# Where a transformer block's SyncE queue issues five kinds of transfers around its first gate-and-up stage

## The chip, the cores and the metric

The kernel runs on one core of a Trainium2 chip as one launch. The metric is the device time in microseconds (us); the kernel before took 1146.49 us as the median of three runs (1145.63 to 1148.01). The engines are TensorE (PE, with its weight loads PEld apart), VectorE (DVE), ScalarE (ACT), GpSimd (POOL) and SyncE (SP). Here SP issues every DMA transfer of the kernel.

## The reference

One transformer block with modulated layer norms, linear attention and a feed-forward part whose weights are 4-bit indices into a table of 16 values. x is 2 x 2048 x 512 in float32, there are 16 heads of 32, and the inner width is 1376.

```python
h = _layernorm(x) * (1 + ca) + sa
q = heads(h @ q_w.T + q_b); k = heads(h @ k_w.T + k_b); v = heads(h @ v_w.T + v_b)
qp = elu(q) + 1; kp = elu(k) + 1
kv = einsum('bhsd,bhse->bhde', kp, v)                  # a sum over the whole sequence
z  = einsum('bhsd,bhd->bhs', qp, kp.sum(axis=2))
x  = x + ga * ((einsum('bhsd,bhde->bhse', qp, kv) / (z + 1e-6)) @ o_w.T + o_b)
h  = _layernorm(x) * (1 + cb) + sb
x  = x + gb * ((silu(h @ lut[gate_idx].T) * (h @ lut[up_idx].T)) @ lut[down_idx].T)
```

sa, ca, ga, sb, cb, gb come from silu(c) @ wmod. Since kv is a sum over the sequence, no row can be finished before every row of its batch has been read once.

## The kernel before

The 4096 rows are cut into 8 groups of 512. Matrices are split into a high and a low half-precision part, and one product is three matmuls: high x high (L1437), high x low (L1438), low x high (L1439). A product of a 128-wide chunk of the inner width with one group is 12 such matmuls of 128x512.

Stage A goes through the 8 groups once for q, k, v and the kv sums, and stores each group's q to `qp_dram`. Then come eight gate-and-up stages `stage_b(s)`, and last a down stage. The inner width has 11 chunks (`FC`), the last of 96 rows. The first stage, s = 0, has 9 chunks (`HELD`), j = 0 to 8 of group 0; below they are called e0 to e8, and e9 on are the chunks of the next stage. Between the chunks of stage s the attention of group s + 1 is finished: its q is divided by z, multiplied with the output weights (`o_piece`, four products of 12 matmuls), normalised and turned (`t_piece`). In stage 0 part of the attention of group 2 is done as well.

One chunk e runs through five engines, each in an order written out by hand:

- PE: 12 matmuls for the gate, 12 for the up product, in banks that alternate with e.
- ACT `silu_gate` (L837): silu of the gate's bank.
- DVE `hid_full` (L1281): `hid_f[e % 2]` = silu times up. It waits for the up product, for silu, and from e2 on for the landing of the store that last read this half of `hid_f`, that of e - 2 (`full_out[e % 2]`).
- ACT `hid_hi` (L845): the high part of `hid_f`; POOL `hid_lo` (L631): the low part.
- SP: a store of `hid_f` to `full_dram` (L496) when `hid_f` is done, and a store of both parts to `hid_dram` (L498) when the low part is done.

Between these stand the attention's instructions. For group 1 in stage 0 they are: DVE `qn_full(1, c)` (L1223) for its four pieces c, ACT `qn_hi` (L776), POOL `qn_lo` (L592). ACT does `qn_hi(1, 2)` and `qn_hi(1, 3)` after `silu_gate` of e3, which stands behind `hid_hi` of e2. POOL does `qn_lo(1, 2)` and `qn_lo(1, 3)` behind `hid_lo` of e2. PE's `o_piece(1, 0)`, behind the up product of e3, waits for all four `qn_lo` of group 1:

```python
if t == 0:
    pe.wait_ge(m_ready, b + 1)
    pe.wait_ge(qn_done, 4 * n + 8)
```

SP's program is one list too, and an instruction of it that waits holds up all that stand behind it. At the end of stage A it stores the last group's q (L402), waits until that store has landed, loads group 2's q (L422) and the output weights for batch 1 (L423), and stores group 0's x after the attention (L427, `x1_store`). Then follow the chunks: before e3's stores the load of the next x into `xg[0]` (L433, `x_next`), and before e4's stores 11 loads of down indices (L474). The first half of `hid_f` is stored again and again under one pair of semaphores:

```python
sp.wait_ge(hid_f_done, e + 1)
if j < FC - 1:
    sp.dma_start(full_dram[g][:, j], hid_f[:, e % 2]).then_inc(full_out[e % 2], 16)
sp.wait_ge(hid_done, e + 1)
sp.dma_start(hid_dram[g][0:m, j], hid[0:m, e % HIDS]).then_inc(hid_out[e % HIDS], 16)
```

Who needs the moved transfers: group 2's q is scaled by ACT `qs_all(2)` (L762) after `hid_hi` of e3; the output weights are read by PE in the middle of stage 1; the x loaded by `x_next(0, 0)` is read by POOL at the start of stage 1; DVE waits for the down indices at the start of stage 2. The down indices go to a part of `w_ffn` that group 0's and group 1's early q and normalised rows use up to e2, so SP waits for those (`x2T_done`, `qn_f_done`) before it loads them.

Of the kernel before, what the change touches and what calls it, by code (L numbers as in the profile page):

```python
# [34 lines left out]
P = 128  # L35
# [13 lines left out]
FC = -(-INTER // P)  # L49
# [30 lines left out]
LOOK_B = [[([(p, False) for p in pieces], first, shares) for pieces, first, shares in stage] for stage in LOOK_B]  # L80
UNITS = [u for units in LOOK_A for u in units] + [u for stage in LOOK_B for units, _, _ in stage for u in units]
EARLY_J = 7


HELD = FC - 2
# [25 lines left out]
def adaln_kernel(nc, x, qwT, qb, kwT, kb, vwT, vb, owT, ob, lut, gateT, upT, downT, cT, wmod, out):  # L111
    with ExitStack() as ctx:
        def sb(name, shape, dt):
            return ctx.enter_context(nc.sbuf_tensor(name, shape, dt))

        def sem(name):
            return ctx.enter_context(nc.semaphore(name))

        def part(arena, start, dt, *dims):

            n = 1
            for d in dims:
                n *= d
            words = n * (2 if dt == F16 else 4) // 4
            v = arena[:, start:start + words]
            if dt != U32:
                v = v.bitcast(dt)
            if len(dims) == 2:
                v = v.rearrange("p (a b) -> p a b", a=dims[0])
            elif len(dims) == 3:  # L130
                v = v.rearrange("p (a b c) -> p a b c", a=dims[0], b=dims[1])
            elif len(dims) == 4:
                v = v.rearrange("p (a b c d) -> p a b c d", a=dims[0], b=dims[1], c=dims[2])
            return v
# [14 lines left out]
        down_idx = w_ffn[:, GU * GROUP:PIECES * GROUP].bitcast(I32).rearrange("p (j n) -> p j n", j=FC)  # L149
# [10 lines left out]
        owt = [qn_words.bitcast(F32).rearrange("p (k n) -> p k n", k=KC), part(arena, 3 * tile_w, F32, KC, HID)]  # L160
# [12 lines left out]
        qp = sb("qp", [P, KC, GROUP], F32)  # L173
# [75 lines left out]
        qp_dram = nc.dram_tensor("qp_dram", (GROUPS, P, KC * GROUP), F32, kind="Internal").ap()  # L249
# [5 lines left out]
        def sems(names):  # L255
            return (sem(n) for n in names.split())
# [3 lines left out]
        idx_in = [sem(f"idx{i}_in") for i in range(5)]  # L260
        raw_in = [sem(f"raw{n}_in") for n in "kvq"]
        mod_in = [sem(f"mod{m}_in") for m in range(6)]
        ow_in = [sem("ow0_in"), sem("ow1_in")]
# [13 lines left out]
        q_neg, q_read, q_act, qp_done, qp_out = sems("q_neg q_read q_act qp_done qp_out")  # L277
# [8 lines left out]
        q_in, qs_done, z_done, z_read, rec_done, spread_done, qn_f_done, qn_hi_done, qn_done = sems(  # L286
            "q_in qs_done z_done z_read rec_done spread_done qn_f_done qn_hi_done qn_done")
        o_done, xob_done, x1_done, stats2_raw, stats2_done, ve2_done, rstd2_done, nmr2_done, xn2_done = sems(
            "o_done xob_done x1_done stats2_raw stats2_done ve2_done rstd2_done nmr2_done xn2_done")
        x2T_done, h2_f_done, h2_done = sems("x2T_done h2_f_done h2_done")  # L290
# [16 lines left out]
        def chunked(w, k=KC):  # L307
            return w.rearrange("(k p) n -> p k n", k=k)

        def flat(v):  # L310
            return v.rearrange("p k n -> p (k n)")
# [4 lines left out]
        def rows_of(j):  # L316
            return P if j < FC - 1 else TAIL
# [35 lines left out]
        def _(sp):  # L353
# [43 lines left out]
            def stage_a(g, par, load):  # L397
                if load:
                    sp.wait_ge(xT_done, 4 * g + 4)
                    sp.dma_start(xg[:, par], xv[g + 2]).then_inc(x_in[par], 16)  # L400
                sp.wait_ge(qp_done, 4 * g + 8)
                sp.dma_start(qp_dram[g], flat(qp[:])).then_inc(qp_out, 16)  # L402
# [15 lines left out]
            sp.wait_ge(xT_done, 4 * 7 + 4)  # L418
            sp.dma_start(xg[:, 1], xv[1]).then_inc(x_in[1], 16)
            stage_a(7, 1, False)  # L420
            sp.wait_ge(qp_out, 16 * 8 + 16)
            sp.dma_start(flat(qp[:]), qp_dram[2]).then_inc(q_in, 16)  # L422
            sp.dma_start(owt[1], chunked(owT)).then_inc(ow_in[1], 16)  # L423

            def x1_store(n, par):
                sp.wait_ge(x1_done, 4 * n + 4)
                sp.dma_start(x1_dram[n], flat(xg[:, par])).then_inc(x1_out[par], 16)  # L427

            def x_next(n, par):
                sp.wait_ge(xn2_done, 4 * n + 4)  # L430
                sp.wait_ge(x1_out[par], 16 * (n // 2 + 1))
                if n + 2 < GROUPS:
                    sp.dma_start(xg[:, par], xv[n + 2]).then_inc(x_in[par], 16)  # L433
                else:
                    sp.dma_start(flat(xg[:, par]), x1_dram[n + 2 - GROUPS]).then_inc(x1_in[par], 16)

            def q_next(n):
                sp.wait_ge(qn_f_done, 4 * n)
                sp.dma_start(flat(qp[:]), qp_dram[n]).then_inc(q_in, 16)

            def full_load(u):
                g, i, cols = u // 2, u % 2, slice(u % 2 * UNIT, u % 2 * UNIT + UNIT)
                if i == 0:
                    for s, count in full_landed(SLOT[(g, FC - 1)]):
                        sp.wait_ge(s, count)
                if u >= 2:
                    sp.wait_ge(left_summed, 4 * (u - 1))
                sp.dma_start(hid_raw[i], full_dram[g][:, :, cols]).then_inc(full_in[i], 16)

            def hid_load(u):  # L450
                g, i, t = u // 2, u % 2, 2 * (u % 2)
                if i == 0:
                    for s, count in landed(SLOT[(g, FC - 1)]):
                        sp.wait_ge(s, count)
                if u >= 2:
                    sp.wait_ge(prod_ready, 7 * (u - 1))
                for which, k, tile in ((S_A11, 0, t), (S_A12, HALF_K, t), (S_A22, HALF_K, t + 1)):
                    sp.dma_start(left[i][which], hid_dram[g][:, k:k + HALF_K, tile]).then_inc(hid_in[i], 16)
                sp.dma_start(left_last[i][0:TAIL], hid_dram[g][0:TAIL, FC - 1, t:t + 2]).then_inc(hid_in[i], 16)

            x1_store(0, 0)
            for s in range(GROUPS):
                n = s + 1
                store, nxt = (6, 7) if s == 0 else (3, 5)
                for i, (g, j) in enumerate(STAGES[s]):
                    e, m = SLOT[(g, j)], rows_of(j)
                    if s == 0 and i == 3:
                        x_next(0, 0)
                    if s == 0 and i == 4:
                        sp.wait_ge(x2T_done, 8)  # L470
                        sp.wait_ge(qn_f_done, 8)
                        for jd in range(FC):
                            md = rows_of(jd)
                            sp.dma_start(down_idx[0:md, jd], downT[jd * P:jd * P + md, :]).then_inc(idx_in[4], 16)  # L474
                    if s < GROUPS - 1:
                        if i == store:
                            x1_store(n, n % 2)
                        if i == nxt:
                            x_next(n, n % 2)
                        if i == 8 and n + 2 < GROUPS:  # L480
                            q_next(n + 2)
                    elif i == 1:
                        sp.wait_ge(up_done, SLOT[(GROUPS - 1, 0)] + 1)
                        hid_load(0)
                    elif i == 5:
                        sp.wait_ge(wf_done, 2 * HALF_K)
                        sp.wait_ge(b_planes, 3 * HALF_K + 1)
                        full_load(0)
                    elif i == 7:
                        sp.wait_ge(up_done, SLOT[(GROUPS - 1, 4)] + 1)  # L490
                        hid_load(1)
                    elif i == 8:
                        full_load(1)
# [5 lines that stand above are left out]
# [930 lines left out]
        def _(pe):  # L1429
# [290 lines left out]
            def gate(g, j):  # L1720
                e = SLOT[(g, j)]
                if j >= EARLY_J:
                    pe.wait_ge(gu_ready, j - EARLY_J + 1)
                if e >= 2:
# [123 lines left out]
```

## Time and profile before

| | before |
|---|---|
| time, median of 3 runs (lowest to highest) | 1146.49 us (1145.63 to 1148.01) |
| the profiled execution's own time | 1147.93 us |
| its span, from the first to the last instruction | 1145.7 us |
| busy: PE, DVE, ACT, POOL | 1105.9, 867.5, 516.8, 370.6 us |
| mean granted TensorE clock | 0.992 |
| the chain that ended last, by engine | PE 84%, DVE 7%, issue 4%, ACT 3% |
| DMA: moved, mean rate over the span | 162.79 MB, 142 GB/s |

The span is what the profile covers; the execution's own time holds some 2 us more. "Busy" of PE counts matmuls, which overlap. The granted clock is the share of full speed at which TensorE was let run. In a timeline, the bracket at a row's end is the time that the engine sat idle before it, and what the profile takes for the releaser; "issue" says that the profile saw none. A transfer's time to landing runs from its issue by SP to the landing of its last part. Stage 0 begins on PE with e0's gate at 355.3 us; DVE multiplies its last chunk, e8, at 432.2 us.

### The profile page before, as it was taken

To read this page: it belongs to the slowest core of one execution; us is meant where nothing else is said; L and a number is where in the kernel's file an instruction comes from. 1 tells how busy PE (TensorE), PEld (TensorE's weight loads), DVE (VectorE), ACT (ScalarE), POOL (GpSimd) and SP (SyncE) were. 2 spreads that over 40 slices of the span, in tenths; PEclk is the share of its full clock that TensorE was granted. 3 is DMA by queue.
4 is the path that set the end of the run, shared out by engine and by line. 5 is a ranking of instruction groups with operands and counts; after the bars stand their busy time and mean duration, and the time that the engine had idled before them with its cause. 6 is when DMAs were issued, how large, how long until landed. Compare 5 with 4: busy or idle time off the path is not lost.

```text
span 1145.7 us, 19116 instructions
## 1 busy us (share of the span) xinstructions
PE 1105.9 (97%) x7508; PEld 610.2 (53%) x7534; DVE 867.5 (76%) x1251; ACT 516.8 (45%) x877; POOL 370.6 (32%) x331
## 2 busy tenths in 40 slices
PE   4899999999999799999999999999999999999998
PEld 2344444544444344444544444444444468888887
DVE  4688988776779568898766987956743968887884
ACT  4667787777726233242421423324224742333231
POOL 1000100002115255474722735726434222222222
PEclk9899999999999899999999999999999999999999
DMA  7930231123112843333322414323242466888872
GB/s 270 324 123 20 89 111 67 46 74 111 37 39 80 276 148 102 138 111 117 127 106 94 157 72 152 113 110 117 76 155 82 158 224 218 257 278 280 272 253 101
DMA packets 115736, 162.79 MB, mean 142 GB/s; under 512 B 7520, under 2 KB 70496, under 8 KB 111552
## 3 DMA queue, kind: packets, MB, share of 16 engines
q1 hardware_dynamic: 115648, 161.58, 41.9%
q8 instruction: 59, 0.97, 0.4%
q14 instruction: 29, 0.24, 0.1%
HBM read 92.88 MB, written 68.68 MB: 141 GB/s over the span
## 4 chain that ended last, share of the span: by engine, by line
PE 84%; DVE 7%; issue 4%; ACT 3%; POOL 1%; DMA 1%; SPq 0%; POOLq 0%; DVEq 0%; ACTq 0%
PE bank L1437 20%; PE bank L1439 20%; PE bank L1438 20%; PE bank L1753 5%; PE bank L1754 5%; PE bank L1755 5%; PE bank L1445 2%; DVE look_buf L1116 2%; PE bank L1589 1%; DMA w_ffn<-in_wmod 1%; DVE w_ffn L1116 1%; PE bank L1507 1%; PE bank L1571 1%; PE bank L1550 1%; PE bank L1757 1%
## 5 line engine op out<-in xcount | busy, mean ns | idle before, releaser
L631 POOL TENSOR_TENSOR shared<-hid_f,shared 128x512 f16<-128x512 f32 (+1 forms) x88 | 117.6, 1336 | 279.2 <-ACT shared L845 279.1
L1437 PE MATMUL bank<-h,w_ffn 128*128 128x512 f16 (+1 forms) x528 | 200.4, 379 | 0.3 <-POOL h L610 0.3
L1438 PE MATMUL bank<-h,w_ffn 128*128 128x512 f16 (+1 forms) x528 | 200.1, 379 | 0.0
L1439 PE MATMUL bank<-h,w_ffn 128*128 128x512 f16 (+1 forms) x528 | 200.1, 379 | 0.0
L845 ACT ACTIVATE shared<-hid_f 128x512 f16<-128x512 f32 (+1 forms) x88 | 55.5, 630 | 249.4 <-DVE hid_f L1281 249.2
L1281 DVE SCALAR_TENSOR_TENSOR hid_f<-bank,sc,shared 128x512 f32<-128x512 f32 (+1 forms) x88 | 65.6, 746 | 100.1 <-PE bank L1439 40.8
L1437 PE MATMUL bank<-arena,h 128*128 128x512 f16 x256 | 98.8, 386 | 5.7 <-issue 2.7
L837 ACT ACTIVATE shared<-bank,sc 128x512 f32<-128x512 f32 (+1 forms) x88 | 60.1, 683 | 96.8 <-PE bank L1439 96.4
L1113 DVE TENSOR_SCALAR look_buf<-look_buf,tab_x,tab 128x512 uint32<-128x512 uint32 x147 | 101.0, 711 | 0.6
L1438 PE MATMUL bank<-arena,h 128*128 128x512 f16 x256 | 98.3, 384 | 0.0
L1439 PE MATMUL bank<-arena,h 128*128 128x512 f16 x256 | 98.3, 384 | 0.0
L639 POOL TENSOR_TENSOR xg<-xg,shared 128x512 f32<-128x512 f32 x32 | 47.7, 1492 | 155.3 <-DVE shared L1353 155.3
L1437 PEld LDWEIGHTS bank<-h,w_ffn 128*128 128x128 f16 (+1 forms) x528 | 52.9, 100 | 66.6 <-issue 8.6
L1116 DVE COPY_PREDICATED look_buf<-look_buf 128x512 uint32<-128x512 uint32 x84 | 85.7, 1020 | 1.2
L1439 PEld LDWEIGHTS bank<-h,w_ffn 128*128 128x128 f16 (+1 forms) x528 | 52.9, 100 | 61.0
L1438 PEld LDWEIGHTS bank<-h,w_ffn 128*128 128x128 f16 (+1 forms) x528 | 52.9, 100 | 57.3 <-issue 0.3
L1116 DVE COPY_PREDICATED w_ffn<-look_buf 128x512 uint32<-128x512 uint32 (+1 forms) x69 | 68.9, 999 | 0.9
L885 ACT ACTIVATE qn_f<-bank,sc 128x256 f32<-128x256 f32 x32 | 14.9, 466 | 120.2 <-PE bank L1755 120.2
L559 POOL TENSOR_SCALAR stats<-stats 128x4 f32<-128x4 f32 x7 | 4.9, 698 | 198.2 <-ACT h L721 198.2
L1437 PE MATMUL bank<-arena,w_ffn 128*128 128x512 f16 (+1 forms) x176 | 66.7, 379 | 0.0
L1438 PE MATMUL bank<-arena,w_ffn 128*128 128x512 f16 (+1 forms) x176 | 66.7, 379 | 0.0
L1439 PE MATMUL bank<-arena,w_ffn 128*128 128x512 f16 (+1 forms) x176 | 66.7, 379 | 0.0
(287 smaller groups left out, 2606.2 us busy)
## 6 DMA issues: line engine op xcount, KB each, us to landing
full_dram<-hid_f SPq DMA_DIRECT2D x80, 256.0 KB, 2.0
hid_dram<-shared SPq DMA_DIRECT2D x80, 256.0 KB, 2.0
w_ffn<-full_dram SPq DMA_DIRECT2D x16, 1280.0 KB, 9.9
xg<-in_x SPq DMA_DIRECT2D x16, 1024.0 KB, 7.0
qp_dram<-qp SPq DMA_DIRECT2D x8, 1024.0 KB, 4.9
x_dram<-xg SPq DMA_DIRECT2D x8, 1024.0 KB, 4.1
xg<-x_dram SPq DMA_DIRECT2D x8, 1024.0 KB, 7.2
qn<-hid_dram SPq DMA_DIRECT2D x24, 320.0 KB, 4.0
```

Source lines behind the costliest of these rows:

```text
L631: pool.tensor_tensor(hid[0:m, e % HIDS, :, 1], whole, hid[0:m, e % HIDS, :, 0], ALU.subtract).then_inc(hid_done, 1)
L837: act.activation(silu_g[0:m, e % 2], bank[2 + 2 * (e % 2)][0:m], ACT.Silu, scale=c1(C_INV_G)[0:m]).then_inc(silu_g_done, 1)
L845: act.activation(hid[0:m, e % HIDS, :, 0], whole, ACT.Copy).then_inc(hid_hi_done, 1)
L1113: ins = dve.tensor_scalar(buf(dst), buf("m0"), tab_x[:, a:a + 1], tab[:, 2 * a:2 * a + 1], ALU.bitwise_and, ALU.bitwise_xor)
L1116: ins = dve.copy_predicated(buf(dst), buf(a), buf(b))
L1281: dve.scalar_tensor_tensor(hid_f[0:m, i], bank[3 + 2 * i][0:m], c1(C_HID)[0:m], silu_g[0:m, i], ALU.mult, ALU.mult).then_inc(hid_f_done, 1)
L1437: pe.matmul(dst, a_hi, b_hi, start=first, stop=False)
L1438: pe.matmul(dst, a_hi, b_lo, start=False, stop=False)
L1439: last = pe.matmul(dst, a_lo, b_hi, start=False, stop=end)
L1753: pe.matmul(dst, l[:, jj, 0], r[:, jj, 0], start=start and jj == 0, stop=False, skip_group_check=True)
L1754: pe.matmul(dst, l[:, jj, 0], r[:, jj, 1], start=False, stop=False, skip_group_check=True)
L1755: last = pe.matmul(dst, l[:, jj, 1], r[:, jj, 0], start=False, stop=end, skip_group_check=True)
```

## The change

Only SP's list changes; PE, DVE, ACT and POOL keep their instructions and their order. A new table `DOWN_LOADS` says before which chunk's stores which down chunks are loaded.

```diff
+DOWN_LOADS = {(0, 5): (0, 1), (0, 6): (2, 3), (0, 7): (4, 5), (0, 8): (6, 7), (1, 0): (8,), (1, 1): (9,), (1, 2): (10,)}
...
             stage_a(7, 1, False)
-            sp.wait_ge(qp_out, 16 * 8 + 16)
-            sp.dma_start(flat(qp[:]), qp_dram[2]).then_inc(q_in, 16)
-            sp.dma_start(owt[1], chunked(owT)).then_inc(ow_in[1], 16)
...
-            x1_store(0, 0)
             for s in range(GROUPS):
                 n = s + 1
                 store, nxt = (6, 7) if s == 0 else (3, 5)
                 for i, (g, j) in enumerate(STAGES[s]):
                     e, m = SLOT[(g, j)], rows_of(j)
-                    if s == 0 and i == 3:
-                        x_next(0, 0)
-                    if s == 0 and i == 4:
-                        sp.wait_ge(x2T_done, 8)
-                        sp.wait_ge(qn_f_done, 8)
-                        for jd in range(FC):
-                            md = rows_of(jd)
-                            sp.dma_start(down_idx[0:md, jd], downT[jd * P:jd * P + md, :]).then_inc(idx_in[4], 16)
+                    if s == 0:
+                        if i == 1:
+                            sp.wait_ge(qp_out, 16 * 8 + 16)
+                            sp.dma_start(flat(qp[:]), qp_dram[2]).then_inc(q_in, 16)
+                        elif i == 2:
+                            x1_store(0, 0)
+                        elif i == 3:
+                            sp.dma_start(owt[1], chunked(owT)).then_inc(ow_in[1], 16)
+                        elif i == 4:
+                            x_next(0, 0)
+                        elif i == 5:
+                            sp.wait_ge(x2T_done, 8)
+                            sp.wait_ge(qn_f_done, 8)
+                    for jd in DOWN_LOADS.get((s, i), ()):
+                        md = rows_of(jd)
+                        sp.dma_start(down_idx[0:md, jd], downT[jd * P:jd * P + md, :]).then_inc(idx_in[4], 16)
```

On SP, from the last store of stage A to the first store of chunk e0, the list stood so before (L402 the last q store, L422 group 2's q, L423 the output weights, L427 group 0's x, L496 and L498 the two stores of e0):

```order
L402 DMA qp_dram<-qp 128x2048
L422 DMA qp<-qp_dram 128x2048
L423 DMA arena<-in_owT 128x4x512
L427 DMA x_dram<-xg 128x2048
L496 DMA full_dram<-hid_f 128x512
L498 DMA hid_dram<-shared 128x1024
```

The same place now, from the last store of stage A (L405) to the first store of chunk e3; line numbers are those of the changed file, in which L503 and L505 are the two stores of a chunk:

```order
L405 DMA qp_dram<-qp 128x2048
L503 DMA full_dram<-hid_f 128x512
L505 DMA hid_dram<-shared 128x1024
L469 DMA qp<-qp_dram 128x2048
L503 DMA full_dram<-hid_f 128x512
L505 DMA hid_dram<-shared 128x1024
L427 DMA x_dram<-xg 128x2048
L503 DMA full_dram<-hid_f 128x512
L505 DMA hid_dram<-shared 128x1024
L473 DMA arena<-in_owT 128x4x512
L503 DMA full_dram<-hid_f 128x512
```

The two stores of e0 moved ahead of three 1 MB transfers, and ahead of SP's wait for the last q store; the stores of e1 stand behind one of the three, those of e2 behind two.

The second place on SP is where the next x and the down indices are loaded. Before, from the load of x (L433) on, chunks e3 and e4:

```order
L433 DMA xg<-in_x 128x4x512
L496 DMA full_dram<-hid_f 128x512
L498 DMA hid_dram<-shared 128x1024
L474 DMA w_ffn<-in_downT 128x512 x10
L474 DMA w_ffn<-in_downT 96x512
L496 DMA full_dram<-hid_f 128x512
```

Now, from the load of x on, chunks e4 to e7 (L481 loads down indices, L427 stores group 1's x, L433 loads the x after it):

```order
L433 DMA xg<-in_x 128x4x512
L503 DMA full_dram<-hid_f 128x512
L505 DMA hid_dram<-shared 128x1024
L481 DMA w_ffn<-in_downT 128x512 x2
L503 DMA full_dram<-hid_f 128x512
L505 DMA hid_dram<-shared 128x1024
L481 DMA w_ffn<-in_downT 128x512 x2
L427 DMA x_dram<-xg 128x2048
L503 DMA full_dram<-hid_f 128x512
L505 DMA hid_dram<-shared 128x1024
L481 DMA w_ffn<-in_downT 128x512 x2
L433 DMA xg<-in_x 128x4x512
```

The 11 loads in one row became two before each of e5 to e8 and one before each of e9 to e11; the load of x stands one chunk later.

## Rows read from the trace of the kernel before

**Rows 1.** The page's part 1: busy us (share of the span) xinstructions.
```profile
PE 1105.9 (97%) x7508; PEld 610.2 (53%) x7534; DVE 867.5 (76%) x1251; ACT 516.8 (45%) x877; POOL 370.6 (32%) x331
```

**Rows 2.** Timeline of PE, e2's gate to e4's: start, us, engine, line, op.
```profile
370.78 0.38 PE L1439 MATMUL bank<-h,w_ffn 128*128 128x512 f16 x1
...
379.71 0.38 PE L1439 MATMUL bank<-h,w_ffn 128*128 128x512 f16 x1
386.66 0.59 PE L1437 MATMUL bank<-arena,qn 128*128 128x512 f16 x1 [6.57 <-issue]
...
391.39 0.38 PE L1437 MATMUL bank<-h,w_ffn 128*128 128x512 f16 x1
...
393.99 0.38 PE L1437 MATMUL bank<-arena,qn 128*128 128x512 f16 x1
```

**Rows 3.** Two stretches: us, busy by engine (x), PEclk, DMA share, GB/s.
```profile
386.66:391.39 4.73, 4.73 (x12) 1.72 (x13) 1.12 (x2) 3.08 (x5) 1.15 (x1) 0.54 0.92 316
421.16:426.00 4.84, 4.84 (x25) 2.47 (x26) 1.49 (x3) 3.19 (x6) 2.24 (x2) 1.00 0.54 171
```

**Rows 4.** Timeline of DVE: the last two pieces of q, then e2's product.
```profile
374.86 0.69 DVE L1223 SCALAR_TENSOR_TENSOR qn_f<-w_ffn,bank 128x512 f32<-128x512 f32 x1 [0.43 <-POOL qn L592]
380.88 0.75 DVE L1281 SCALAR_TENSOR_TENSOR hid_f<-bank,sc,shared 128x512 f32<-128x512 f32 x1 [5.34 <-DMA full_dram<-hid_f]
```

**Rows 5.** Timeline of SP's queue: issue, us that the issue took.
```profile
367.17 0.34 SPq L422 DMA_DIRECT2D qp<-qp_dram  x1
...
368.57 0.77 SPq L496 DMA_DIRECT2D full_dram<-hid_f  x1
...
390.13 6.22 SPq L474 DMA_DIRECT2D w_ffn<-in_downT  x11
```

**Rows 6.** DMA issues of 362 to 384 us: KB each, median us to landing.
```profile
qp<-qp_dram SPq DMA_DIRECT2D x1, 1024.0 KB, 4.8
arena<-in_owT SPq DMA_DIRECT2D x1, 1024.0 KB, 8.8
...
full_dram<-hid_f SPq DMA_DIRECT2D x3, 256.0 KB, 12.1
```

**Rows 7.** The page's part 6, whole span: the same store.
```profile
full_dram<-hid_f SPq DMA_DIRECT2D x80, 256.0 KB, 2.0
```

**Rows 8.** Timeline of ACT, e2's silu to the scaling of group 2's q.
```profile
371.20 0.69 ACT L837 ACTIVATE shared<-bank,sc 128x512 f32<-128x512 f32 x1 [2.27 <-PE bank L1439]
...
381.67 0.63 ACT L845 ACTIVATE shared<-hid_f 128x512 f16<-128x512 f32 x1 [8.75 <-DVE hid_f L1281]
382.21 0.67 ACT L837 ACTIVATE shared<-bank,sc 128x512 f32<-128x512 f32 x1
382.77 1.14 ACT L776 ACTIVATE qn<-qn_f 128x512 f16<-128x512 f32 x2
...
388.35 2.55 ACT L762 ACTIVATE qp<-qp,ksq 128x512 f32<-128x512 f32 x4
```

**Rows 9.** Timeline of POOL in the same stretch.
```profile
372.48 2.27 POOL L592 TENSOR_TENSOR qn<-qn_f,qn 128x512 f16<-128x512 f32 x2 [2.32 <-ACT qn L776]
382.38 1.33 POOL L631 TENSOR_TENSOR shared<-hid_f,shared 128x512 f16<-128x512 f32 x1 [7.62 <-ACT shared L845]
383.67 2.89 POOL L592 TENSOR_TENSOR qn<-qn_f,qn 128x512 f16<-128x512 f32 x2
```

**Rows 10.** Timeline of PE: two other idle times, in stage A and stage 0.
```profile
39.95 0.63 PE L1437 MATMUL bank<-arena,h 128*128 128x512 f16 x1 [2.71 <-issue]
...
421.16 0.66 PE L1445 MATMUL bank<-ident,arena 128*128 128x128 f32 x4 [1.40 <-POOL arena L605]
```

**Rows 11.** The store of e7 alone (line L496, 425.2 to 425.6 us).
```profile
L496 SPq DMA_DIRECT2D full_dram<-hid_f x1: 319/319/319, 425.3 to 425.3; - x1
...
DMA to landing us min/median/max: 3.6/3.6/3.6
```

**Rows 12.** Timeline of DVE: e9's product, two chunks after that store.
```profile
438.52 0.73 DVE L1281 SCALAR_TENSOR_TENSOR hid_f<-bank,sc,shared 128x512 f32<-128x512 f32 x1
```

## The prediction

> **What bounds the kernel now.** I read the page's busy times first: PE is busy in 97% of the span [rows 1], so only PE's idle time, and the time in which it runs slowly, can move the end. Second came PE's timeline, stretch by stretch, to list its idle times. After stage A has begun in earnest there are few, and one stands out [rows 2]: the up product of e3 ends at 379.71 + 0.38 = 380.09 us, and the next matmul, the first of `o_piece(1, 0)`, starts at 386.66. The reader is to see the bracket of 6.57 us, and that the 12 matmuls of that product take 391.39 - 386.66 = 4.73 us, where the next 12 take 393.99 - 391.39 = 2.60. Third, the stretches by granted clock: it is 0.54 for those 12 and 1.00 at 421 us [rows 3], so they ran mostly at 1.2 GHz and not at 2.4, after an idle engine. So one place costs 6.57 + 2.13 = 8.70 us.
>
> "Issue" names no cause, so I went back along the program. `o_piece(1, 0)` waits for the last `qn_lo` on POOL, which ends at 383.67 + 2.89 = 386.56, 0.10 before PE starts [rows 9]. It waited for ACT's `qn_hi` at 382.77, that stood behind `hid_hi` of e2 at 381.67 [rows 8], and that waited for DVE's product of e2 at 380.88. DVE had been free since 374.86 + 0.69 = 375.55 and sat idle for 5.34 us until a DMA landed [rows 4]: the store of e0's `hid_f`. SP issued it at 368.57, after it had waited until 367.17 for the last q store and had then issued three transfers of 1 MB [rows 5]. It took 12.1 us to land, behind them [rows 6], where the median of all 80 such stores is 2.0 [rows 7]: 368.57 + 12.1 = 380.7, and DVE starts at 380.88.
>
> **The change, part by part.** *Stores of e0 ahead of the burst.* SP now issues e0's store as soon as e0's product is done, before it waits for the q store. That product precedes 367.17 (SP found it done). In front of the store is only the last q store, and that had landed by 367.17. So e0's store lands at the latest a little after 367.17 + 2.0 = 369.2, against the 375.55 at which DVE wants it: the 5.34 us go. Bounds: with the 12.1 us of before, from about 364 it would be 376.1, a wait of 0.6.
>
> What is late next, step by step. DVE begins e2's product at 375.6; its up product ended 24 matmuls before e3's, at 380.09 - 2 x 2.60 = 374.9, so PE is not the limit. ACT's `hid_hi` follows 0.79 later (381.67 - 380.88), at 376.4, and ends by 377.0. `silu_gate` of e3 then waits for e3's gate, which ends at 380.09 - 2.60 = 377.5; on e2 ACT began 0.04 after the gate's end (371.20 against 370.78 + 0.38), so ACT is there at 377.5 instead of 382.21. The `qn_hi` pair begins 0.56 after it (382.77 - 382.21), at 378.1, and the first of the two ends half of 1.14 later, at 378.7. POOL has `hid_lo` of e2 from 377.1 (0.71 after `hid_hi`) to 378.4, so its `qn_lo` pair begins at about 378.8, with 0.1 for the handoff. The pair took 2.27 at 372.48 and 2.89 at 383.67 [rows 9]. I take 2.89, since DVE's table lookups run beside it as they did there; 2.27 is the other end. It ends at 381.7, and PE starts at 381.8: 4.9 us earlier than 386.66, with an idle time of 1.7 left. At the other end it is 5.5.
>
> *The clock.* An idle time of 1.40 at 421.16 was followed by a stretch at 1.00 [rows 3, 10]; one of 2.71 at 39.95 was followed by matmuls of 0.63 us, as at 386.66, against 0.38 [rows 2, 10]. 1.7 is nearer to 1.40, so I take the clock as kept: 2.13 us are saved, at the other end nothing.
>
> *Stores of e1 and e2.* e1's store stands behind group 2's q (1 MB, 4.8 us to landing [rows 6]), issued at 367.17 as before. It lands at about 374, and even with 12.1 us at about 381. The product of e3 wants it when e3's up product is done, at 380.1, and DVE's lookups run until about 382: no cost at either end. e2's stores stand behind group 0's x, which SP issues at about 370.7; two chunks later there is ample room.
>
> *Output weights before e3, next x before e4.* e3's store is issued behind the output weights, which took 8.8 us beside two other transfers [rows 6]. e5's product is two chunks and three products of `o_piece` after e3's: seven times 2.60, some 18 us, against 12.1. No cost. The next x is issued behind the landed x store, that SP waits for; SP reaches it after e3's low part, some 13 us after that store's issue, more than 12.1.
>
> *Down loads in pairs.* The 11 loads took SP 6.22 us to issue and held up nothing that PE waited for [rows 5]; taking them apart gives nothing. They now stand before the stores of e5 to e11. The tightest store I found is e7's: issued at 425.3, landed in 3.6 us [rows 11], wanted by e9's product at 438.52 [rows 12], 13.2 us after its issue. Two loads are 0.5 MB; the 3.25 MB of the burst took from 367.17 to 380.7, so 0.5 MB are about 2.1 us. 5.7 against 13.2: no cost. Each later time is shifted alike on all engines, since from 386.66 on they wait for PE.
>
> *Issuing later.* Group 2's q leaves SP at 367.17 as before, lands at 367.17 + 4.8 = 372.0, and ACT takes it up at 388.35 [rows 8], after the change at about 383. It stays early by some 10 us. The Trainium skill, DMA: Bandwidth & Descriptors, in Rules for kernel authors, says to issue a DMA early and to wait on it late, which speaks against moving loads back. By that rule alone the sum would be 0 or a loss, and it is weighed as the last rival below; the trace differs here, since the early burst is what DVE's 5.34 us waited behind.
>
> **The sum.** 4.9 + 2.1 = 7.0 us. The profiled execution took 1147.93 us, with a span of 1145.7: it would take 1140.9. It was 1.4 us above the median of 1146.49, so in terms of the median I forecast 1139.5 us.
>
> **The rivals.**
> - *The clock falls all the same.* The 1.7 us left are more than the 1.40 that did no harm, and some step of the chain may be slower than I took it. Then the gain is 4.9 and the time 1141.6; with an idle time of 2.7, 3.9 and 1142.6. For it: 2.71 was enough once. Against: the steps are measured ones.
> - *The idle time goes entirely*, if POOL's pair is fast and ACT overlaps more: 8.7 us, 1137.8. Against it: e3's gate ends at 377.5, and four steps follow it.
> - *Nothing changes.* e0's store still lands late, or another wait of the same length takes its place, since POOL or SP is later than I think: about 1146.5. Against: it would have to land 11 us after its issue, with one transfer in front of it.
> - *Slower: the paired loads make landings late in several chunks.* Place: DVE's products of e8 to e11, which wait for stores that now have down loads, an x store, an x load or a q load in front of them. The point from which it decides is 13.2 us to landing. At 16 us each of four chunks would lose 2.8, 11.2 in all, and with the 7.0 saved the time is 1150.7. Against: 5.7 was worked out, and the stores that had 3 MB in front took 12.1.
>
> **How the numbers follow.** Forecast 0.71, clock falls 0.13, idle gone 0.08, nothing changes 0.04, slower 0.04. The first three are faster, 0.92 together; 0.2% is 2.3 us, about what a measurement here can tell from no change. The range goes from 1137.4, which is the case without idle time less 0.4 for the spread of runs, to 1142.4, which takes in most of the case with the low clock; outside are the last two and a part of the second, under 0.2.
>
> **What would show it.** In the profile after: e0's store issued at about 364 and landed by 370; no DVE idle time on a DMA before e2's product, which starts at about 375.6; PE's idle time before `o_piece(1, 0)` at 1 to 2 us and its 12 matmuls in 2.6 us at a granted clock of 1.00; the idle time of 1.40 before `t_piece(1, 0)` as before, some 7 us earlier. I am wrong if DVE waits for a landing at e3, e8, e9 or e10, if PE's 12 matmuls still take 4.7 us, or if PE gets a new idle time later in stages 0 and 1.

## The result, and the profile after

The changed kernel took 1138.94 us as the median of four runs (1138.04 to 1141.27), against 1146.06 us of the kernel before in the four runs taken by then (1145.07 to 1148.01). The ratio is 0.9939, with a 95% interval of 0.9918 to 0.9960: faster by 7.1 us, where 7.0 were forecast (1139.5 us in terms of the median). The profiled execution took 1141.27 us with a span of 1139.0.

PE after the change, from the end of e3's up product on (columns as before: start, us, engine, line; L1444 to L1446 are the L1437 to L1439 of before):

```profile
379.94 0.38 PE L1446 MATMUL bank<-h,w_ffn 128*128 128x512 f16 x1
382.11 0.38 PE L1444 MATMUL bank<-arena,qn 128*128 128x512 f16 x1 [1.80 <-issue]
...
384.70 0.38 PE L1444 MATMUL bank<-h,w_ffn 128*128 128x512 f16 x1
...
414.47 0.65 PE L1452 MATMUL bank<-ident,arena 128*128 128x128 f32 x4 [1.40 <-POOL arena L612]
```

These answer to [rows 2]: the idle time of 6.57 us is down to 1.80, and the 12 matmuls of `o_piece(1, 0)` take 384.70 - 382.11 = 2.59 us instead of 4.73. The idle time of 1.40 before `t_piece(1, 0)` [rows 10] is still there, 6.7 us earlier. The granted clock of the same stretches, against [rows 3], where the first had 0.54 (columns: stretch, us, then busy time of PE, PEld, DVE, ACT, POOL, granted clock, DMA share, GB/s):

```profile
382.11:384.70 2.59, 2.59 (x13) 1.17 (x13) 0.00 (x0) 2.59 (x5) 1.16 (x1) 1.00 0.94 361
414.47:419.00 4.53, 4.53 (x24) 2.35 (x24) 1.19 (x3) 2.88 (x5) 2.22 (x2) 1.00 0.56 176
```

SP's queue, answering to [rows 5], and the landing of e0's store of `hid_f` alone. It answers to the 12.1 us of [rows 6], which is the median of three stores; e0's alone took 12.2 before:

```profile
363.51 0.34 SPq L405 DMA_DIRECT2D qp_dram<-qp  x1
364.18 0.34 SPq L503 DMA_DIRECT2D full_dram<-hid_f  x1
...
367.42 0.32 SPq L469 DMA_DIRECT2D qp<-qp_dram  x1
368.51 0.32 SPq L503 DMA_DIRECT2D full_dram<-hid_f  x1
```

```profile
L503 SPq DMA_DIRECT2D full_dram<-hid_f x1: 338/338/338, 364.2 to 364.2; - x1
...
DMA to landing us min/median/max: 3.9/3.9/3.9
```

It leaves SP at 364.18, as soon as e0's product is done, and lands at 368.1. In the kernel before, the last q store left at 363.30 and e0's product was done just as early, at 363.19 + 0.74 = 363.93, but SP issued the store only at 368.57 [rows 5]:

```profile
363.30 0.34 SPq L402 DMA_DIRECT2D qp_dram<-qp  x1
```

```profile
363.19 0.74 DVE L1281 SCALAR_TENSOR_TENSOR hid_f<-bank,sc,shared 128x512 f32<-128x512 f32 x1
```

```profile
L496 SPq DMA_DIRECT2D full_dram<-hid_f x1: 773/773/773, 368.6 to 368.6; - x1
...
DMA to landing us min/median/max: 12.2/12.2/12.2
```

So, counted from the issue of the last q store, the landing comes 12.9 us sooner: 4.6 because the store is issued sooner, 8.3 because it lands sooner after its issue. DVE, answering to [rows 4], no longer waits:

```profile
375.08 0.69 DVE L1230 SCALAR_TENSOR_TENSOR qn_f<-w_ffn,bank 128x512 f32<-128x512 f32 x1 [0.43 <-POOL qn L599]
375.68 0.75 DVE L1288 SCALAR_TENSOR_TENSOR hid_f<-bank,sc,shared 128x512 f32<-128x512 f32 x1
...
380.93 0.73 DVE L1288 SCALAR_TENSOR_TENSOR hid_f<-bank,sc,shared 128x512 f32<-128x512 f32 x1
```

And the steps behind it, ACT's (`hid_hi` of e2, `silu_gate` of e3, the `qn_hi` pair) and POOL's (`hid_lo` of e2, the `qn_lo` pair), against [rows 8, 9]:

```profile
376.46 0.63 ACT L852 ACTIVATE shared<-hid_f 128x512 f16<-128x512 f32 x1 [3.32 <-DVE hid_f L1288]
377.76 0.69 ACT L844 ACTIVATE shared<-bank,sc 128x512 f32<-128x512 f32 x1 [0.67 <-PE bank L1446]
378.35 1.14 ACT L783 ACTIVATE qn<-qn_f 128x512 f16<-128x512 f32 x2
```

```profile
377.17 1.35 POOL L638 TENSOR_TENSOR shared<-hid_f,shared 128x512 f16<-128x512 f32 x1 [2.19 <-ACT shared L852]
379.04 2.97 POOL L599 TENSOR_TENSOR qn<-qn_f,qn 128x512 f16<-128x512 f32 x2 [0.52 <-ACT qn L783]
```

What the reader is to see is the releaser of `silu_gate`: it is now PE, so the chain starts at e3's gate product, and POOL's pair ends at 382.01, 0.10 before PE goes on.

Spans are hard to compare directly, since stage A's start differs by up to 3 us between executions: the last q store leaves SP at 360.58 to 363.51 us in the profiles of this study. So I take the time from that store to the end of the span. Before it is 1145.7 - 363.3 = 782.4, after it is 1139.0 - 363.5 = 775.5: 6.9 us. The two terms read above are (6.57 - 1.80) + (4.73 - 2.59) = 4.77 + 2.14 = 6.91, the same within the 0.1 us to which spans are given.

### The profile page after: what moved, and what is told of

It reads as the page before. It is cut to its first block, busy times and chain, and to the rows that moved or that the text cites. A ratio compares the mean times of both kernels' runs of the same rounds, so it can differ in the third digit from the quotient of the medians.

```text
span 1139.0 us, 19142 instructions
## 1 busy us (share of the span) xinstructions
PE 1106.0 (97%) x7534; PEld 609.5 (54%) x7534; DVE 866.5 (76%) x1251; ACT 517.1 (45%) x877; POOL 370.6 (33%) x331
## 4 chain that ended last, share of the span: by engine, by line
PE 85%; DVE 7%; issue 3%; ACT 3%; POOL 1%; DMA 1%; SPq 0%; POOLq 0%; DVEq 0%; ACTq 0%
PE bank L1444 20%; PE bank L1446 20%; PE bank L1445 20%; PE bank L1760 5%; PE bank L1761 5%; PE bank L1762 5%; PE bank L1452 2%; DVE look_buf L1123 2%; PE bank L1596 1%; DMA w_ffn<-in_wmod 1%; DVE w_ffn L1123 1%; PE bank L1514 1%; PE bank L1578 1%; PE bank L1557 1%; PE bank L1764 1%
## 5 line engine op out<-in xcount | busy, mean ns | idle before, releaser
L1444 PE MATMUL bank<-h,w_ffn 128*128 128x512 f16 (+1 forms) x528 | 200.4, 379 | 0.2 <-POOL h L617 0.2
L1446 PE MATMUL bank<-h,w_ffn 128*128 128x512 f16 (+1 forms) x528 | 200.1, 379 | 0.0
L1444 PE MATMUL bank<-arena,h 128*128 128x512 f16 x256 | 98.9, 386 | 2.1 <-DVE h L1029 1.1
L1446 PE MATMUL bank<-arena,h 128*128 128x512 f16 x256 | 98.3, 384 | 0.0
L1444 PEld LDWEIGHTS bank<-h,w_ffn 128*128 128x128 f16 (+1 forms) x528 | 52.9, 100 | 66.8 <-issue 8.6
L1446 PEld LDWEIGHTS bank<-h,w_ffn 128*128 128x128 f16 (+1 forms) x528 | 52.9, 100 | 61.1
L1444 PE MATMUL bank<-arena,w_ffn 128*128 128x512 f16 (+1 forms) x176 | 66.7, 379 | 0.0
L1446 PE MATMUL bank<-arena,w_ffn 128*128 128x512 f16 (+1 forms) x176 | 66.7, 379 | 0.0
```

Of the source, the lines that this page charges most:

```text
L1444: pe.matmul(dst, a_hi, b_hi, start=first, stop=False)
L1446: last = pe.matmul(dst, a_lo, b_hi, start=False, stop=end)
```

## The experiments

The runs are numbered 1 to 9, while e0, e1 and so on stay the names of chunks. Each run was timed in turn with the kernel before. The table gives the ratio to it with the 95% interval, and from each profile DVE's wait for the store of e0, PE's idle time before `o_piece(1, 0)`, the time of its 12 matmuls, and the time from the last q store to the end. The first two rows are the kernels before and after. The edits of runs 1, 6, 7 and 9 are shown against the changed kernel, the others against the kernel before.

| kernel | ratio | DVE waits | PE idle | 12 matmuls | q store to end |
|---|---|---|---|---|---|
| before | 1 | 5.34 | 6.57 | 4.73 | 782.4 |
| after | 0.9939 [0.9918, 0.9960] | 0 | 1.80 | 2.59 | 775.5 |
| run 1, first burst alone | 0.9949 [0.9936, 0.9962] | 0 | 1.80 | 2.59 | 775.5 |
| run 2, down loads alone | 0.9996 [0.9987, 1.0005] | 5.06 | 6.29 | 4.83 | 782.3 |
| run 3, e0's stores first | 0.9944 [0.9930, 0.9958] | 0 | 1.80 | 2.59 | 775.6 |
| run 4, 2 MB ahead | 0.9938 [0.9927, 0.9950] | 1.36 | 2.62 | 2.59 | 776.3 |
| run 8, 2.5 MB ahead | 0.9990 [0.9980, 1.0000] | 3.82 | 5.04 | 4.22 | 780.4 |
| run 5, on ACT's queue | 0.9944 [0.9932, 0.9956] | 0.72 | 2.41 | 2.59 | 776.1 |
| run 9, down loads before e7 | 0.9932 [0.9918, 0.9946] | 0 | 1.78 | 2.59 | 775.5 |

In every row the last column is 775.5 plus what idle time and matmuls have over 1.80 and 2.59, within 0.1 us. The ratios of runs 1, 3, 4, 5, 9 and of the changed kernel cannot be told apart; by their profiles, one of each, runs 1, 3 and 9 are like the changed kernel, and runs 4 and 5 are 0.8 and 0.6 us slower. Runs 6 and 7 are below.

**Run 1: the first burst alone dealt out.**

```diff
-DOWN_LOADS = {(0, 5): (0, 1), (0, 6): (2, 3), ...
+DOWN_LOADS = {(0, 4): tuple(range(FC))}
...
+                        if i == 3:
+                            x_next(0, 0)
                         elif i == 4:
-                            x_next(0, 0)
-                        elif i == 5:
                             sp.wait_ge(x2T_done, 8)
```

> Only the first burst is dealt out (group 2's q before e1, group 0's x before e2, output weights before e3); the next x stands before e3 and the 11 down loads in a row before e4, as in the kernel before. Theory (all of the gain comes from e0's stores no longer standing behind 3 MB): as the changed kernel, 1138.9 us, PE idle before o_piece(1, 0) 1.8 us at a granted clock of 1.00. Rival (the second burst costs something too): 1 to 3 us slower than the changed kernel, with a new idle time of DVE on a landing at e5 or e6.

Measured: 1141.11 us against 1147.62 of the kernel before, and the same 775.5 as after. DVE waits for no landing at e5 or e6. The times alone would not exclude the rival's loss of 1 us, since the ratios 0.9949 and 0.9939 have intervals that overlap; the profile does, and by it the theory holds.

**Run 2: the down loads alone dealt out**, with the load of the next x moved as in the change.

```diff
-                    if s == 0 and i == 3:
+                    if s == 0 and i == 4:
                         x_next(0, 0)
-                    if s == 0 and i == 4:
+                    if s == 0 and i == 5:
                         sp.wait_ge(x2T_done, 8)
                         sp.wait_ge(qn_f_done, 8)
-                        for jd in range(FC):
...
+                    for jd in DOWN_LOADS.get((s, i), ()):
```

> Only the second burst is dealt out (next x before e4, down loads in pairs from e5 on); the first burst stays ahead of e0's stores. Theory: as the kernel before, 1146.1 us within 0.2%, PE idle 6.6 us before o_piece(1, 0), DVE idle 5.3 us on the landing of e0's store. Rival (the second burst costs something): 1 to 3 us faster than before.

Measured: 1146.51 against 1147.62, no difference. DVE before e2's product, and PE before `o_piece(1, 0)`:

```profile
379.32 0.75 DVE L1282 SCALAR_TENSOR_TENSOR hid_f<-bank,sc,shared 128x512 f32<-128x512 f32 x1 [5.06 <-DMA full_dram<-hid_f]
```

```profile
385.11 0.58 PE L1438 MATMUL bank<-arena,qn 128*128 128x512 f16 x1 [6.29 <-issue]
```

The stall is as it was. The half of the change that moves the most transfers is worth nothing.

**Run 3: the first burst kept whole, but behind e0's stores.**

```diff
-            sp.wait_ge(qp_out, 16 * 8 + 16)
-            sp.dma_start(flat(qp[:]), qp_dram[2]).then_inc(q_in, 16)
-            sp.dma_start(owt[1], chunked(owT)).then_inc(ow_in[1], 16)
...
-            x1_store(0, 0)
...
+                    if s == 0 and i == 1:
+                        sp.wait_ge(qp_out, 16 * 8 + 16)
+                        sp.dma_start(flat(qp[:]), qp_dram[2]).then_inc(q_in, 16)
+                        sp.dma_start(owt[1], chunked(owT)).then_inc(ow_in[1], 16)
+                        x1_store(0, 0)
```

> The first burst is kept whole, as three transfers in a row with the wait for the last q store ahead of them, but e0's two stores stand ahead of it instead of behind it; all else as in the kernel before. Theory (one store's place is the whole effect): as the changed kernel, 1139 us; e0's store lands by 369; e1's and e2's stores, now behind 3 MB, land at about 381, when e3's product is ready anyway (e3's product at 381, e4's at 393). Rival (spreading is what helps, since the burst now delays e1's store): DVE waits for e1's store until about 381.5 and later work slips, 1141 to 1146 us.

Measured: 1140.32 against 1147.62. This is the clearest of the runs, since the burst is untouched. e1's store now stands behind the 3 MB and lands as late as e0's did; then DVE's products of e2 and e3:

```profile
L497 SPq DMA_DIRECT2D full_dram<-hid_f x1: 602/602/602, 366.1 to 366.1; - x1
...
DMA to landing us min/median/max: 12.2/12.2/12.2
```

```profile
372.91 0.75 DVE L1282 SCALAR_TENSOR_TENSOR hid_f<-bank,sc,shared 128x512 f32<-128x512 f32 x1
...
378.36 0.75 DVE L1282 SCALAR_TENSOR_TENSOR hid_f<-bank,sc,shared 128x512 f32<-128x512 f32 x1
```

The landing at 366.1 + 12.2 = 378.3 comes just ahead of e3's product at 378.36. The same 12.2 us that cost 7 us on e0's store cost nothing on e1's. Dealing out is not what helps; the place of e0's stores is.

**Runs 4 and 8: how much stands ahead of e0's stores.** Run 4 stores group 0's x behind them; run 8 in place of that loads the second half of the output weights behind them, between the stores of e0 and e1.

```diff
-            x1_store(0, 0)
             for s in range(GROUPS):
...
+                    if s == 0 and i == 1:
+                        x1_store(0, 0)
```

```diff
-            sp.dma_start(owt[1], chunked(owT)).then_inc(ow_in[1], 16)
+            sp.dma_start(owt[1][:, 0:2], chunked(owT)[:, 0:2]).then_inc(ow_in[1], 16)
...
+                    if s == 0 and i == 1:
+                        sp.dma_start(owt[1][:, 2:4], chunked(owT)[:, 2:4]).then_inc(ow_in[1], 16)
...
-                    pe.wait_ge(ow_in[b], 16)
+                    pe.wait_ge(ow_in[b], 16 + 16 * b)
```

> The kernel before with two transfers of 1 MB ahead of e0's stores in place of three (group 0's x is stored behind e0's stores). A dose: 3.25 MB took from 367.2 to 380.8, so 2.25 MB take 9.4 us. Theory: e0's store lands at about 376.6 to 377.5, DVE idle 1 to 2 us before e2's product, PE idle 2.8 to 3.8 us before o_piece(1, 0), which is 1 to 2 us over the 1.8 of the changed kernel; with the clock kept 1140 to 1141 us, with the clock lost for one product 1142 to 1143. Rival (the wait does not go with the bytes in front): 1139 or 1146.

> The kernel before, with the second half of the output weights' load (0.5 MB) behind e0's stores, so 2.5 MB stand ahead of them; 2 MB gave DVE 1.36 us and PE 2.62 us of idle time, 3 MB gave 5.34 and 6.57. Theory (the wait goes with the bytes in front): DVE idle 3.0 to 3.7 us, PE idle 4.2 to 5.0. If the clock is kept after that, 2.7 us slower than the changed kernel, 1141.6; if it falls for o_piece(1, 0), 4.2 to 4.9 slower, 1143 to 1144. Rival (steps, not bytes): as with 2 or with 3 transfers.

Measured: run 4 1140.35 against 1147.62, run 8 1144.97 against 1146.65. DVE and PE of run 4, then of run 8, with the stretch of run 8's 12 matmuls:

```profile
375.38 0.75 DVE L1282 SCALAR_TENSOR_TENSOR hid_f<-bank,sc,shared 128x512 f32<-128x512 f32 x1 [1.36 <-DMA full_dram<-hid_f]
```

```profile
381.18 0.38 PE L1438 MATMUL bank<-arena,qn 128*128 128x512 f16 x1 [2.62 <-issue]
```

```profile
378.26 0.75 DVE L1283 SCALAR_TENSOR_TENSOR hid_f<-bank,sc,shared 128x512 f32<-128x512 f32 x1 [3.82 <-DMA full_dram<-hid_f]
```

```profile
384.04 0.59 PE L1439 MATMUL bank<-arena,qn 128*128 128x512 f16 x1 [5.04 <-issue]
```

```profile
384.04:388.26 4.22, 4.22 (x12) 1.55 (x13) 1.11 (x2) 3.07 (x5) 1.15 (x1) 0.60 0.80 304
```

The wait goes with the bytes ahead: e0's store lands 8.8, 10.7 and 12.2 us after its issue, and DVE waits 1.36, 3.82 and 5.34 us, at 2, 2.5 and 3 MB. SP's wait for the last q store alone is not the cause, for in runs 4 and 8 it still stands ahead of e0's store. Run 4 came within its expectation but for PE's idle time, 0.2 below it. In run 8 both idle times came out slightly above what I expected (3.0 to 3.7 and 4.2 to 5.0), and with them the loss against the changed kernel: 780.4 - 775.5 = 4.9 us, at the upper end of the 4.2 to 4.9 expected. Here the longer idle time cost more than its length: after 2.62 us the matmuls start 0.22 apart as ever, after 5.04 the first eight run at 1.2 GHz, and 1.63 us are lost to that beside the idle time. In time run 8 is close to the kernel before, and its interval reaches 1.0000; the runs alone do not show a gain, and its size is read from the profile, 780.4 against 782.4.

**Run 5: e0's store on ACT's queue, no sooner than before.** SP counts a semaphore up once it has issued the three transfers, and ACT waits for that; SP leaves this one store out.

```diff
+            sp.sem_inc(burst_issued, 1)
...
-                    if j < FC - 1:
+                    if j < FC - 1 and e:
...
+                    if s == 0 and i == 1:
+                        act.wait_ge(hid_f_done, 1)
+                        act.wait_ge(burst_issued, 1)
+                        act.dma_start(full_dram[0][:, 0], hid_f[:, 0]).then_inc(full_out[0], 16)
```

> The kernel before, with one store issued elsewhere: e0's store of hid_f goes out on ACT's queue, and not before SP has issued its three transfers of 1 MB, so the same 3 MB are under way and only the queue differs. Theory as the prediction had it (a store lands behind the bytes that were issued before it, whoever issues it): it lands after about 12 us, DVE idle 5 us, 1146 us. Rival (it waits only behind what stands in its own queue, and the 16 DMA engines serve both queues in turn): it lands in 2 to 5 us, DVE does not wait, PE idle 1.8 us before o_piece(1, 0), 1139 to 1140 us; e1's store stays behind the burst and costs nothing.

Measured: 1139.57 against 1146.65. The issues of 362 to 386 us (KB each, median us to landing), and DVE's product of e2:

```profile
x_dram<-xg SPq DMA_DIRECT2D x1, 1024.0 KB, 12.6
...
full_dram<-hid_f ACTq DMA_DIRECT2D x1, 256.0 KB, 7.9
```

```profile
374.02 0.75 DVE L1287 SCALAR_TENSOR_TENSOR hid_f<-bank,sc,shared 128x512 f32<-128x512 f32 x1 [0.72 <-DMA full_dram<-hid_f]
```

Both expectations missed the landing, though the time is within the rival's. The store leaves ACT 5.4 us after the last q store, where SP issued it 5.3 after it before, and lands after 7.9 us, neither 12 nor 2 to 5, which leaves DVE 0.72 us of waiting. So of the 10.2 us by which the landing of 12.2 exceeded the median 2.0 [rows 7], 4.3 went with the store's place in SP's own queue, and 5.9 stayed on another queue beside the same traffic; that these are a wait for the DMA engines, which both queues use, is my reading. Those 4.3 were most of DVE's wait, since DVE wants the landing only some 7 us after the issue. The Trainium skill, DMA: Bandwidth & Descriptors, in Queues, rings and completion order, says that each engine takes packets from its queues in turn; a landing between the two agrees, and no run here shows the turns themselves.

**Run 9: all down loads in a row before e7's stores**, to try the prediction's slower rival at the point where the least room is left. In the changed kernel e7's store is issued at 418.59 and takes 9.3 us to land, where the prediction had 5.7, and e9's product starts at 432.00:

```profile
L503 SPq DMA_DIRECT2D full_dram<-hid_f x1: 326/326/326, 418.6 to 418.6; - x1
...
DMA to landing us min/median/max: 9.3/9.3/9.3
```

```profile
432.00 0.73 DVE L1288 SCALAR_TENSOR_TENSOR hid_f<-bank,sc,shared 128x512 f32<-128x512 f32 x1
```

```diff
+DOWN_LOADS = {(0, 7): tuple(range(FC))}
...
-                        elif i == 5:
+                        elif i == 7:
                             sp.wait_ge(x2T_done, 8)
```

> The changed kernel, but all 11 down loads stand in a row before e7's stores, ahead of the load of the next x, to see what a late landing costs at e9. In the changed kernel e7's store is issued at 418.6, lands after 9.3 us, and e9's product wants it 13.4 us after its issue. Bytes in front of it grow from 1.5 to 3.75 MB; at 0.24 MB a us it lands 15 to 18 us after its issue. Theory (the prediction's slower rival, as a mechanism): DVE idles 2 to 5 us before e9's product on that landing, and as DVE is nearly full until e10, PE waits before o_piece(2, 2): 1 to 4 us slower than the changed kernel. Rival (PE is two chunks ahead of what it needs of e9): DVE idles as much, PE does not, and the time is that of the changed kernel.

Measured: 1139.07 against 1147.75, the time of the changed kernel. SP's queue, and DVE's product of e9:

```profile
413.07 5.36 SPq L481 DMA_DIRECT2D w_ffn<-in_downT  x11
418.53 0.39 SPq L433 DMA_DIRECT2D xg<-in_x  x1
418.96 0.94 SPq L503 DMA_DIRECT2D full_dram<-hid_f  x1
```

```profile
428.89 0.74 DVE L1288 SCALAR_TENSOR_TENSOR hid_f<-bank,sc,shared 128x512 f32<-128x512 f32 x1
```

No wait, so neither side of the expectation was tested. Two things were mis-sized. The room was 9.9 us and not 13.4: e7's product was done at 415.64, but SP was issuing the 11 loads, 5.36 us long, and issued the store only at 418.96, while DVE wanted it at 428.89. And the store landed after 9.6 us, at 428.6, where 15 to 18 were expected; the loads had been under way since 413.07, which the count left out. What it costs when DVE waits at e9 stays open; that a burst of 2.7 MB may stand there at no cost is shown, with 0.3 us to spare.

**Runs 6 and 7: the idle times that are left.** Run 6 is the changed kernel with `o_piece(1, 0)` behind the gate product of e4 (its edit below); run 7 has `t_piece(1, 0)` behind the up product of e7 as well.

```diff
-                    b_attn = {0: [lambda: z_sum(1)], ... 4: [lambda: o_piece(1, 1)],
+                    b_attn = {0: [lambda: z_sum(1)], ... 4: [lambda: o_piece(1, 0), lambda: o_piece(1, 1)],
-                    a_attn = {..., 3: [lambda: o_piece(1, 0)], 4: [lambda: o_piece(1, 2)],
+                    a_attn = {..., 4: [lambda: o_piece(1, 2)],
```

> The changed kernel, and on PE o_piece(1, 0) moved from before the gate product of e4 to behind it. Theory (the 1.8 us left before o_piece(1, 0) are a wait for POOL's qn_lo that 2.6 us of matmuls can cover): that idle time goes, 1.8 us less than the changed kernel, ratio to the kernel before 0.992 to 0.993. Rival (the work comes late for what follows, x1_tile(1, 0) and o_piece(1, 2)): the idle time shows up again before o_piece(1, 2) and the time is that of the changed kernel.

> As the run before, and t_piece(1, 0) moved from before the up product of e7 to behind it. Theory: the idle time of 1.40 us before t_piece(1, 0) is covered too, 3.2 us less than the changed kernel, ratio to the kernel before 0.991 to 0.992. Rival: ACT's h_b(1, 0) starts later and e7's high part behind it, so an idle time of 1 us or more shows up at e8 or e9 and 1.8 us are left of the gain.

Measured: run 6 1136.88 against 1146.65, ratio 0.9919 [0.9906, 0.9932]; run 7 1136.60, ratio 0.9918 [0.9905, 0.9931]. PE's first matmul of `o_piece(1, 0)` in run 6 has no idle time before it, and the next idle time in run 6 is the old one before `t_piece(1, 0)`; in run 7 that is gone, and two late starts are left in the first product of stage 1:

```profile
380.78 0.38 PE L1444 MATMUL bank<-arena,qn 128*128 128x512 f16 x1
...
410.55 0.66 PE L1452 MATMUL bank<-ident,arena 128*128 128x128 f32 x4 [1.41 <-POOL arena L612]
```

```profile
419.80 0.38 PE L1446 MATMUL bank<-h,w_ffn 128*128 128x512 f16 x1
420.23 0.39 PE L1444 MATMUL bank<-h,w_ffn 128*128 128x512 f16 x1
...
420.67 0.38 PE L1446 MATMUL bank<-h,w_ffn 128*128 128x512 f16 x1
421.34 0.39 PE L1444 MATMUL bank<-h,w_ffn 128*128 128x512 f16 x1 [0.29 <-POOL h L617]
```

From the last q store to the end run 6 takes 1135.0 - 361.55 = 773.4 us and run 7 1133.6 - 360.58 = 773.0, against 775.5. Run 6 gives back 2.1 us where 1.8 were expected. Run 7 adds 0.4 of the 1.4 expected. About 0.7 came back as the two late starts, 0.43 and 0.67 us after the matmul before, where 0.22 is usual (the bracket counts only the time in which no matmul was busy). Another 0.4 went in the down stage, where run 7's lead over run 6 falls from 0.8 to 0.4 us; why is open. By the profiles both beat the kernel before and the changed one; by the times run 6 and the changed kernel have intervals that overlap, and run 7 against run 6 is not settled.

## Why the prediction was right

*The cause* was right: e0's store waited behind 3 MB, and through DVE, ACT and POOL PE waited for it. Run 3 shows it by moving e0's two stores alone, run 2 by leaving them in place, runs 4 and 8 by the dose; run 5 moves the `hid_f` store alone and leaves the other in SP's queue. One premise was not in the rows, that e0's product is done before 367.17; the row of 363.19 above shows it.

*The stall's size* was right: 4.9 us forecast, 4.77 measured. The next limit was named rightly, e3's gate product and the four steps behind it. POOL's pair took 2.97 us, where I chose 2.89 over 2.27, and the idle time left is 1.80 where 1.7 was worked out.

*The clock* came out: 2.1 us forecast, 2.14 measured. It was the least certain term, and its ground did not hold: the length of the idle time was to decide, with 1.40 on one side and 2.71 on the other. The 2.71 was really about 2.3, since a matmul's record is missing there, and the same 2.3 kept the clock in other runs (last section). At this place the clock was kept after 1.80, 2.41 and 2.62 and lost after 5.04, so the term had room; that much was luck.

*The stores of e1 and e2* were at no cost, as argued; run 3 puts e1's store at the worst landing, and the argument still holds, by 0.1 us. *Down loads and later issue* cost nothing (run 1 against the changed kernel).

*What was off.* The room at e9's product: I forecast 5.7 us to landing out of 13.2, and it was 9.3 out of 13.4. The load of the next x left SP only 1.62 us ahead of e7's store, where it was 2.61 before, since two down loads stand before it; I had added their bytes to the 3.6 of before and not counted that. That is 1.0 of the 3.6 us that were missing; the rest stays open. It cost nothing, but the margin was 4.1 us and not 7.5. In run 1, with the down loads in a row before e4, e7's store landed in 3.4 us: dealing them out gained nothing and cut the margin there from 9.8 to 4.1 us. And a store's wait is not set by the bytes issued before it alone: in run 5 another queue took 4.3 us off it.

## What to carry to other kernels

In a queue that several kinds of transfers share, look for the small store whose landing a two-buffer scheme waits for, and put it ahead of large loads that nobody needs yet; that was worth 7 us here, and dealing out 2.7 MB of other loads nothing. When PE's idle time goes, go along the released chain to the next limit before counting it all, and add what PE loses at 1.2 GHz after the stall. Where the start of an execution varies by about as much as the effect, compare profiles from a fixed event near the change to the end.

## What the runs showed of the hardware that I had not expected

- On ACT's queue a store of 256 KB landed in 7.9 us beside 3 MB in SP's queue, where in SP's queue behind them it took 12.2.
- The length of an idle time alone did not decide on the clock. In stage 0 it was kept after 2.62 us (run 4). At one place in stage A, the changed kernel's matmuls ran at 1.2 GHz after 2.33 us, where run 4 seems to have kept the clock after 2.54 (the changed kernel first, then run 4):

```profile
39.72 0.59 PE L1500 MATMUL bank<-shared 128*128 128x512 bf16 x1 [2.33 <-issue]
```

```profile
39.88 0.38 PE L1438 MATMUL bank<-arena,h 128*128 128x512 f16 x1 [2.54 <-issue]
```

In run 4's profile, and in that of the kernel before with its 2.71 [rows 10], the first matmul after the idle time has no record. The weight loads have theirs (the changed kernel, run 4, the kernel before), and by them the three idle times are the same:

```profile
39.69 0.10 PEld L1500 LDWEIGHTS bank<-shared 128*128 128x128 bf16 x1 [2.79 <-issue]
```

```profile
39.63 0.10 PEld L1494 LDWEIGHTS bank<-shared 128*128 128x128 bf16 x1 [2.79 <-issue]
```

```profile
39.55 0.10 PEld L1493 LDWEIGHTS bank<-shared 128*128 128x128 bf16 x1 [2.79 <-issue]
```

From 39.7 to 42.7 us the granted clock was 0.51 in the changed kernel, 0.50 in the kernel before and 1.00 in run 4, after the same instructions and the same idle time. What made the difference no run shows.
- SP took longer to issue a store right behind much else: 0.94 us for e7's store behind 11 loads and the 1 MB of x in run 9, and 0.77 for e0's behind three transfers of 1 MB before, against 0.32 to 0.34 for most others. That the bytes ahead are the reason is not shown.
